# Conv phases of a graph network: the message products of a group's two halves and the bias additions of the next group's filters in turn on VectorE

## What is computed

```python
for i in range(DEPTH):
    W = ssp(rbf @ fw1[i] + fb1[i]) @ fw2[i] + fb2[i]
    W = W * C[:, None]
    h = x @ lin1_w[i]
    msg = h[src] * W
    agg = jax.ops.segment_sum(msg, dst, num_segments=n) / denom
    x = x + ssp(agg) @ lin2_w[i] + lin2_b[i]
    mu = jnp.mean(x, axis=-1, keepdims=True)
    var = jnp.mean((x - mu) ** 2, axis=-1, keepdims=True)
    x = (x - mu) * jax.lax.rsqrt(var + 1e-05) * ln_g[i] + ln_b[i]
```

## Time and profile before

| what | value |
|---|---|
| median of three runs | 4510.42 us (4504.89 to 4515.02) |
| profiled execution, its own time | 4507.14 us |
| its span, from the first to the last instruction | 4505.3 us |
| GpSimd busy | 3299.8 us (73%) |
| TensorE busy | 2503.2 us (56%) |
| ScalarE busy | 2154.4 us (48%) |
| VectorE busy | 1969.7 us (44%) |

### The profile page before, as it was taken

How to read it: one execution, slowest core, us unless ns; L and a number is a source line. 1 busy time by engine, 2 the same in 40 slices (tenths; PEclk the granted TensorE clock), 3 DMA queues, 4 the chain that set the end, 5 groups by cost and what they waited for, 6 DMA issues and landing times. The chain is left out here.

```text
span 4505.3 us, 53247 instructions
## 1 busy us (share of the span) xinstructions
PE 2503.2 (56%) x13164; PEld 2231.5 (50%) x13164; DVE 1969.7 (44%) x4501; ACT 2154.4 (48%) x5585; POOL 3299.8 (73%) x3337
## 2 busy tenths in 40 slices
PE   3444556666566665666656666566763333333343
PEld 3444455556456554655546555456652333323333
DVE  4121155555555555555555555666662222221111
ACT  3434356665556655565556665566654454510000
POOL 5777767777677776777767777777775777757776
PEclk7555567777677776777767776676665555555555
DMA  6333222222222222222222222222221222212221
GB/s 135 92 97 97 76 63 68 67 70 57 61 68 69 69 57 63 66 70 67 57 64 67 70 68 54 64 69 67 67 54 42 55 57 55 55 43 55 57 56 53
DMA packets 193619, 297.21 MB, mean 66 GB/s; under 512 B 81669, under 2 KB 116194, under 8 KB 193302
## 3 DMA queue, kind: packets, MB, share of 16 engines
q0 software_dynamic: 106496, 219.17, 18.9%
q10 hardware_dynamic: 33974, 57.75, 4.4%
q1 hardware_dynamic: 52832, 16.73, 1.5%
HBM read 272.15 MB, written 21.27 MB: 65 GB/s over the span
## 5 line engine op out<-in xcount | busy, mean ns | idle before, releaser
L608 POOL DMA_INDIRECT rows<-table,staged_src x3328 | 3298.8, 991 | 1196.2 <-issue 890.1
L780 PE MATMUL pD<-scatter,msg 128*128 128x80 f32 x4160 | 757.9, 358 | 712.3 <-PEq L778 712.2
L780 PEld LDWEIGHTS pD<-scatter,msg 128*128 128x128 f32 x4160 | 715.2, 267 | 785.1 <-issue 785.0
L701 PE MATMUL pD<-scatter,rows 128*128 128x80 f32 x2496 | 572.0, 424 | 684.5 <-PEq L693 407.4
L772 PE MATMUL pC<-fw,hidden 128*128 (+1 forms) x4160 | 812.6, 371 | 181.2 <-PEq L770 179.7
L701 PEld LDWEIGHTS pD<-scatter,rows 128*128 128x128 f32 x2496 | 545.6, 331 | 707.3 <-issue 707.2
L772 PEld LDWEIGHTS pC<-fw,hidden 128*128 128x128 f32 x4160 | 757.2, 279 | 217.3 <-issue 216.6
L918 ACT ACTIVATE scatter<-onehot,c_e 128x80 f32<-128x80 bf16 x2080 | 549.4, 346 | 589.4 <-ACTq L916 589.4
L1351 DVE TENSOR_TENSOR msg<-msg,rows 128x512 f32<-128x512 f32 x520 | 337.0, 689 | 728.6 <-DVEq L1148 710.7
L1144 DVE COPY staged_src<-src_i 128x8 int32<-128x8 int32 x416 | 72.5, 174 | 691.4 <-DVEq L1156 691.4
L951 ACT ACTIVATE hidden<-hidden 128x512 f32<-128x512 f32 x520 | 327.5, 630 | 62.3 <-ACTq L843 1.6
(11 more groups left out here) (197 smaller groups left out, 1791.4 us busy)
## 6 DMA issues: line engine op xcount, KB each, us to landing
rows<-table,staged_src POOLq DMA_INDIRECT x3328, 2.5
basis<-basis_d ACTq DMA_DIRECT2D x130, 256.0 KB, 2.8
table<-node_rows SPq DMA_DIRECT2D x66, 128.0 KB, 1.8
msg<-in_edge_weight_dram ACTq DMA_DIRECT2D x54, 128.0 KB, 3.1
basis_d<-basis ACTq DMA_DIRECT2D x26, 256.0 KB, 3.8
hidden<-in_edge_weight_dram ACTq DMA_DIRECT2D x48, 128.0 KB, 3.2
table<-node_rows SPq DMA_DIRECT2D x11, 132.0 KB, 2.3
out_dram<-node_rows SPq DMA_DIRECT2D x11, 128.0 KB, 1.8
```

The lines of the kernel that those rows point to most:

```text
L608: pool.indirect_dma_start(out=rows[:, s, j, 0:width], out_offset=None, in_=tab[:, :], in_offset=bass.IndirectOffsetOnAxis(ap=staged_src[:, ...
L701: mm = pe.matmul(sum_ps, rows[:, g % RING, j, 0:D], scatter[:, g % 2, j, :], start=(j == 0), stop=(j == CH - 1))
L780: mm = pe.matmul(sum_ps, msg_of(g, h)[:, c * D:(c + 1) * D], scatter[:, g % 2, HALF * h + c, :], start=(h == 0 and c == 0), stop=(h == 1 a ...
```

## The change

`take_filters` takes one half of a group instead of both. In the loop of a conv phase the addition for the first half of the next group moves between the two products of the group; the addition for the second half stays behind the staging copy. Before the loop both halves of group 0 are taken as they were.

```diff
-                def take_filters(l, g):
-                    for h in range(2):
-                        dve.wait_ge(filt_full, 1)
...
+                def take_filters(l, g, h):
+                    dve.wait_ge(filt_full, 1)
...
-                        take_filters(l, 0)
+                        take_filters(l, 0, 0)
+                        take_filters(l, 0, 1)
...
                             messages(g, 0)
+                            take_filters(l, g + 1, 0)
                             messages(g, 1)
                             stage(g)
-                            take_filters(l, g + 1)
+                            take_filters(l, g + 1, 1)
```

More of the change, by code:

```diff
@@ L1339, in softplus_rest @@
                                                  ALU.max, ALU.add).then_inc(ssp_full, 1)
-                def take_filters(l, g):
-                    for h in range(2):
-                        dve.wait_ge(filt_full, 1)
[L1344 to L1347, removed]
+                def take_filters(l, g, h):
+                    dve.wait_ge(filt_full, 1)
+                    dve.sem_inc(filt_full, -1)
+                    dve.tensor_tensor(msg_of(g, h).rearrange("p (c d) -> p c d", d=D),
+                                      filt_ps[h].rearrange("p (c d) -> p c d", d=D),
+                                      over_tiles(fb2[:, l, :], HALF), ALU.add).then_inc(filt_free, 1)
                 def messages(g, h):
```

## The result

The changed kernel takes 4497.2 us (median of 8 runs, 4492.2 to 4500.6), the kernel before 4511.5 us in the runs beside it (8 runs). The ratio is 0.9968, with a 95% interval of 0.9957 to 0.9979: 14.3 us faster, where 20 were forecast (4490, range 4475 to 4503). The profiled execution's span went from 4505.3 to 4490.3 us.

A forecast was written before the change was run, and what follows sets the result against it. GpSimd's gathers were taken as the bound. 27.9 us gross less 10.3 give-back is 17.6; replays gave 18 and 22; 20 was taken. Profiled 4507.1 less 20 is 4487, plus 3.3 for the median: 4490 us, range 4475 to 4503.

The forecast's parts named there:

- The bound: GpSimd's 3328 row gathers at L608 set the time; VectorE waits for their rows, so its own savings are worth nothing.
- the rule: A gather starting during a VectorE operation with two SBUF inputs lasts 0.94 us plus time to that operation's end less 0.125.
- The rival of the copy: The staging copy, not the second product, stretches the gather it falls into; no change, 4510 us; chance 0.05.
- The gross gain: In the five conv stretches the second product no longer runs across a gather's start (223 times before): 27.9 us saved.
- The give-back: Gathers start earlier, so 96 matches running across a gather's start stretch it more: 10.3 us of the saving lost.
- the 17.6 us by hand: Net gain in the five conv stretches: 27.9 us saved less 10.3 us that the match takes back.
- the two replays: The five stretches' 2080 gathers recomputed with the 0.94 us and 0.125 us formula, old and new order: 22 or 18 us less.
- the second replay: Recomputed gathers, what waits for ScalarE's logarithms keeping its distance from the group before: 18 us less, match share up 11.
- the first replay: Recomputed gathers, every operation keeping its distance from its own group's product 0: 22 us less, match share up 6.
- up to 1.8 us more gain: At the conv stretches' ends the last group's first product may miss a gather start: at most 5 x 0.35 us.
- Cover: The next group's filters are ready 2.7 us before addition 0, so the wait now between the products costs nothing.

The follow-up runs named there:

- The run with one input: Kernel before, the second product of groups 0 to 50 replaced by a sum with one input in SBUF: 4487.5 us, ratio 0.9970.
- the copy's run: Kernel before with only the staging copy moved, behind the first addition, the two products left side by side: 4501.8 us, ratio 1.0009.
- the first pair of traces: Traces of the kernel before and the changed kernel as first measured: 4511.5 and 4497.2 us, ratio 0.9968.
- the pair on one chip: Kernel before and changed kernel measured again, both on one chip: 4512.0 and 4496.8 us, ratio 0.9966.
- The run with the added copy: Kernel before plus one small copy on VectorE between a group's rows and its first product, in 255 rounds: 4514.6 us, ratio 1.0005.

## Why the prediction came out as it did

**The bound and the rule held.** GpSimd's pauses between gathers are as they were (890.2 us), and what was won is gather time. The rule foretold the gather lengths in each row above to 0.02 us, and for the 358 gathers that products, matches and the operations on y hold in the trace before it misses by at most 0.015 us. The run with one input shows that a sum with one input in SBUF does not hold a gather where a product with two does; L1518 shows that two are not always needed. The sentence of the Trainium skill (SBUF — State Buffer, "Who interferes with whom") that infers no hindrance of descriptor writing by a tensor_tensor cannot be carried over to a whole gather: 0 us by it, 30.5 us of stretch gone here. Whether the writing of descriptors is held, or the reading of the offsets in `staged_src`, no run here shows. The rival of the copy fell with the copy's run.

**The gross gain** was put at 27.9 us and is 30.5: no second product lengthens a gather any more (seven begin up to 0.003 us before one, without effect), and the trace before has five more gathers that begin just as the first product ends and the second has begun, 2.6 us, which the prediction had not counted.

**The give-back** was 10.3 us by hand for the match; it measured 10.8 us in the first pair of traces and 4.7 us in the pair on one chip. It is not the match alone: the node mean and value took back another 2.8 us in the first pair, which the prediction did not price. So it is in part luck that the 17.6 us by hand lie so near the 18.2 measured: 2.6 us too little gain and 2.8 us too little give-back cancel.

**What was mis-sized.** I had 17.6 us, 18 and 22 from the two replays, and took 20, the middle. The stretches lost 18.2 us, which is the second replay, in which what waits for ScalarE keeps its distance from the group before (18 us), and its 11 us for the match against 10.8. The run with the added copy also has a match that does not keep its distance from its own product. But in the pair on one chip the match took 4.7 us, nearer the first replay's 6, so which replay is right is not shown.

**What was missing.** At a phase's end I allowed up to 1.8 us more gain and priced no loss. My reading of VectorE's 0.35 us there as a wait for the last rows was wrong: it is 0.35 us in the row after too, though the last gather then ends 2.51 us ahead of that product (1683.77 to 1686.28) instead of 1.90 (1691.45 to 1693.35). The last gather before:

```profile
1690.51 0.94 POOL L608 DMA_INDIRECT rows<-table,staged_src  x1 [0.30 <-issue]
```

The last group's first product did miss the gather's start, as the rows of the kernel after show; VectorE and GpSimd at that place, which answer to the earlier trace rows:

```profile
1681.60 0.71 DVE L1350 TENSOR_TENSOR msg<-msg,rows 128x512 f32<-128x512 f32 x1
...
1686.28 0.69 DVE L1350 TENSOR_TENSOR msg<-msg,rows 128x512 f32<-128x512 f32 x1 [0.35 <-DVEq L1152]
```

```profile
1681.58 0.95 POOL L608 DMA_INDIRECT rows<-table,staged_src  x1 [0.30 <-issue]
1682.83 0.94 POOL L608 DMA_INDIRECT rows<-table,staged_src  x1 [0.30 <-issue]
1700.32 4.05 POOL L608 DMA_INDIRECT rows<-table,staged_src  x1 [16.54 <-POOLq L606]
```

The gather takes 0.95 instead of 1.43 us, but the wait for the next table grew from 15.92 to 16.54 us: the last two gathers end 0.5 us sooner in front of a chain on VectorE that does not. The 18.2 us of stretch contain some 2.4 us of this kind that were never on the path. The waits at the ends grew by 2.7 us in all, so 18.2 - 2.7 = 15.5 us stand against 14.3 to 15.2 measured, and the forecast of 20 was 2 too high from the choice of the middle and 3 from the ends.

**Cover held.** The additions waited 7.8 us in all after, 7.4 before: the wait that moved between the products costs nothing.

## What to carry to other kernels

Where GpSimd issues gathers and is the bound, count the gathers that are longer than the shortest and look at what VectorE runs when they start; a VectorE operation may be worth moving though VectorE itself has time to spare. Fix all the operations that cross at once, by lengths against the gather's beat: a single one that is moved shifts the beat against the others, and they give part of it back or take more. Before a stretch's saving is put down as gain, subtract what lies in front of a chain that does not get shorter.

## What the runs showed of the hardware that was not expected

A gather is held when a VectorE operation with two inputs in SBUF has begun before it and is still running; its 0.94 us then count from 0.125 us before that operation's end. Products that had begun only 0.04 us before a gather, or less, did nothing (5 times before, 11 times after). A sum with one such input, 0.68 us long, does nothing (203 crossings, 0.0 us), nor does an addition with its other input in PSUM (431 crossings); the maximum over `deg` at L1518, a tensor_scalar with one tile as input, does hold a gather (2.46 us). A 3.49 us operation so costs up to 3.1 us, pieces of 0.75 us cost the gathers 0.2 to 0.6 us each. And two chips differ by 13 us in the unchanged kernel, of which some 10 may come from 46 ns between a group's last gather and its first product.
